# The tail of a cross-attention and mixture-of-experts kernel: four additions made into steps of their own, and the routing of two token groups moved up

## What is computed

```python
x = x + xattn(ctx, layernorm(x))          # 16 heads of 64, 1101 keys for each of 2 sequences of 1024
h = layernorm(x)                          # 2048 tokens of 256
shared = silu(h @ sg) * (h @ su) @ sd     # hidden width 512
# routing: l2-normed h against 8 group and 32 expert centroids
_, top_group_idx = top_k(group_scores, 4)
top_scores, top_idx = top_k(masked, 4)
gates = softmax(top_scores)
pos = cumsum(onehot, axis=0)[..., flat_e] - 1     # place of a token in its expert's list, capacity 320
buf[e, pos] = h[tok]
out_e = (silu(buf @ wg) * (buf @ wu)) @ wd        # 32 experts
routed[tok] += out_e * gate
out = x + shared + routed
```

## Time and profile before

| what | value |
|---|---|
| median of 3 runs | 1611.84 us (1609.86 to 1613.97) |
| the profiled execution | 1614.24 us, span 1612.5 us |
| mean granted TensorE clock | 0.984 |
| TensorE busy (matmuls) | 1503.6 us, 93% |
| VectorE busy | 1043.6 us, 65% |
| ScalarE busy | 796.2 us, 49% |
| POOL busy | 940.4 us, 58% |

### The profile page before, as it was taken

How to read it: one execution, slowest core, us unless ns; L and a number is a source line. 1 busy time by engine, 2 the same in 40 slices (tenths; PEclk the granted TensorE clock), 3 DMA queues, 4 the chain that set the end, 5 groups by cost and what they waited for, 6 DMA issues and landing times.

```text
span 1612.5 us, 23811 instructions
## 1 busy us (share of the span) xinstructions
PE 1503.6 (93%) x8086; PEld 1059.1 (66%) x8086; DVE 1043.6 (65%) x1574; ACT 796.2 (49%) x1501; POOL 940.4 (58%) x751
## 2 busy tenths in 40 slices
PE   4799999999999999999999999988989999999995
PEld 4465665555655665566555565546889999999995
DVE  6557556676676665767767776556756666666662
ACT  3455445444554455444554445433436666666663
POOL 4567756666677676765768768882534333343333
PEclk9999999999999999999999999998999999999998
DMA  3034430000000000000001011002256666666664
GB/s 107 11 81 96 101 81 15 10 15 10 25 15 10 15 11 24 15 11 15 24 18 32 24 41 33 31 31 69 87 172 189 178 168 176 182 189 180 168 177 90
DMA packets 99282, 117.93 MB, mean 73 GB/s; under 512 B 10595, under 2 KB 78181, under 8 KB 99173
## 3 DMA queue, kind: packets, MB, share of 16 engines
q1 hardware_dynamic: 82149, 96.97, 20.6%
q0 software_dynamic: 17056, 19.97, 6.3%
HBM read 74.93 MB, written 35.06 MB: 68 GB/s over the span
## 4 chain that ended last, share of the span: by engine, by line
PE 75%; DVE 16%; POOL 3%; ACT 3%; issue 2%; DMA 1%; SPq 0%; DVEq 0%; POOLq 0%; ACTq 0%
PE ps_o L965 14%; PE ps_t L822 9%; PE ps_m L822 8%; PE ps_m L927 8%; PE ps_st L822 7%; DVE arena_r L1325 7%; PE ps_st L950 6%; PE ps_st L954 6%; PE ps_m L859 3%; PE ps_o L859 3%; PE ps_t L985 2%; PE ps_t L1032 2%; PE ps_t L972 2%; DVE arena L1336 2%; POOL arena L762 2%
## 5 line engine op out<-in xcount | busy, mean ns | idle before, releaser
L762 POOL TENSOR_TENSOR arena<-arena 128x512 f32<-128x512 f32 (+1 forms) x512 | 660.8, 1292 | 321.7 <-ACT arena L1608 284.0
L1608 ACT ACTIVATE arena<-ps_st 128x512 f32<-128x512 f32 (+1 forms) x576 | 330.0, 597 | 457.5 <-PE ps_st L954 444.8
L1325 DVE TENSOR_REDUCE arena_r<-ps_m 128x1 fp32r<-128x1107 f32 x256 | 334.1, 1305 | 189.2 <-PE ps_m L927 187.0
L797 POOL DMA_INDIRECT acc_rows<-arena,ids x96 | 150.8, 1570 | 268.2 <-ACT arena L1671 240.5
L965 PE MATMUL ps_o<-arena 128*64 128x512 f32 (+1 forms) x1152 | 275.2, 603 | 0.0
L950 PE MATMUL ps_st<-arena_r 128*128 128x512 f32 (+1 forms) x576 | 246.3, 428 | 2.7 <-ACT arena L1608 2.6
L954 PE MATMUL ps_st<-arena_r 68*128 68x512 f32 (+2 forms) x576 | 230.8, 401 | 3.2 <-DVE arena_r L1332 2.1
L927 PE MATMUL ps_m<-arena_r 128*128 128x370 f32 x768 | 190.7, 357 | 36.4 <-DVE arena_r L1325 32.6
L927 PEld LDWEIGHTS ps_m<-arena_r 128*128 128x128 f32 x768 | 131.0, 191 | 102.2 <-DVE arena_r L1325 84.0
L950 PEld LDWEIGHTS ps_st<-arena_r 128*128 128x128 f32 (+1 forms) x576 | 106.6, 185 | 102.3 <-ACT arena L1608 68.2
L822 PE MATMUL ps_m<-arena_r 128*128 128x320 f32 (+1 forms) x864 | 165.2, 327 | 2.1 <-DVE arena_r L1415 1.2
(11 more groups left out here) (212 smaller groups left out, 1860.1 us busy)
## 6 DMA issues: line engine op xcount, KB each, us to landing
arena<-in_L_ffn_wg_dram SPq DMA_DIRECT2D x32, 512.0 KB, 4.6
arena<-in_L_ffn_wu_dram SPq DMA_DIRECT2D x32, 512.0 KB, 6.0
arena<-in_L_ffn_wd_dram SPq DMA_DIRECT2D x32, 512.0 KB, 3.9
x_slots<-route SPq DMA_DIRECT2D x5, 2176.0 KB, 12.9
arena<-x_slots SPq DMA_DIRECT2D x32, 272.0 KB, 2.7
arena_r<-arena_r SPq DMA_DIRECT2D x30, 275.2 KB, 3.6
arena<-in_L_xattn_Wkv_dram SPq DMA_DIRECT2D x32, 128.0 KB, 2.4
arena<-x_slots SPq DMA_DIRECT2D x32, 68.0 KB, 2.4
```

Of the source, the lines that this page charges most:

```text
L762: pool.tensor_tensor(total, probsT[0:rows, h, 0, :] if kt == 1 else total, probsT[0:rows, h, kt, :], ALU.add).then_inc(added, 1)
L797: pool.indirect_dma_start(out=dst[:, :], in_=y_sb[par][:, c, 0:w], in_offset=None, compute_op=ALU.add, out_offset=bass.IndirectOffsetOnAxi ...
L1325: dve.tensor_reduce(neg[h][:, c:c + 1], ps_m[:, :, 0:PIECE_W], AX.XY, ALU.max, negate=True)\
L1608: act.activation(probsT[0:rows, h, kt, :], ps_st[0:rows, n % 2, :], ACT.Exp).then_inc(exp_done, 1)
```

## The change

The four additions of a chunk become events `acc c,i` of their own, placed by hand in the list. For group 2, everything from `top` to `places_b` moves up; the norm of group 3 and its transposes move ahead of chunk 0's `down`; the additions of chunk 0 stand between routing steps of group 2; `pos` of group 2 now comes ahead of `score` of group 3. For group 3, `gexp`, `hot_*`, `pos`, `gates`, `places_*` and the scatters move ahead of chunk 1's `down`. No instruction is added or taken away. The code, with the long lists cut to two lines:

```diff
+    def sums(c):
+        return [("acc", c, i) for i in range(4)] + [("accout", c)]
+
-    def last(c):
+    def last(c, between=[]):
         return [("high", c, HIDS - 1), ("lowh", c, HIDS - 1)] + \
                ([("up", c + 1, 0), ("silu", c + 1, 0), ("hid", c + 1, 0)] if c < NCHUNKS - 1 else []) + \
-               [("down", c), ("accout", c)]
+               between + [("down", c)] + sums(c)
...
+             ("pos", 2), ("low", 3, 0), ("low", 3, 1), ("silu", 1, 0), ("acc", 0, 0), ("acc", 0, 1), ("gates", 2),
+             ("acc", 0, 2), ("places_a", 2), ("acc", 0, 3), ("accout", 0), ("places_b", 2), ("norm_c", 3),
...
+    tail += last(1, [("pos", 3), ("gates", 3), ("places_a", 3), ("places_b", 3)] + scats[3]) + hidden(2, 1)
...
-                if kind == "down":
-                    for i in range(4):
-                        jn = JOB["y", a, i]
-                        job_filled(dve, jn)
-                        t = a * GT + i
-                        dve.tensor_tensor(x_sb[:, t, :], bank_of(jn)[:, 0:D], x_sb[:, t, :], ALU.add)\
-                           .then_inc(free_of(jn), 1)
+                if kind == "acc":
+                    jn = JOB["y", a, ev[2]]
+                    job_filled(dve, jn)
+                    t = a * GT + ev[2]
+                    dve.tensor_tensor(x_sb[:, t, :], bank_of(jn)[:, 0:D], x_sb[:, t, :], ALU.add)\
+                       .then_inc(free_of(jn), 1)
```

More of the change, by code:

```diff
@@ L260, in whole_plan @@
                  ("hid", 0, 1), ("up", 0, 2), ("score", 2)] + outs
[L261 to L272, removed]
+    tail += [("silu", 0, 2), ("high", 0, 0), ("lowh", 0, 0), ("scored", 2), ("top", 2), ("hid", 0, 2), ("ws", 2), ("wl", 2),
+             ("stat_a", 3), ("stat_b", 3), ("up", 0, 3), ("root", 3), ("high", 0, 1), ("lowh", 0, 1),
+             ("mask_a", 2), ("mask_b", 2), ("silu", 0, 3), ("high", 0, 2), ("lowh", 0, 2), ("hid", 0, 3),
+             ("best_a", 2), ("best_b", 2), ("high", 0, 3), ("lowh", 0, 3), ("hot_a", 2), ("hot_b", 2), ("hot_c", 2),
+             ("gexp", 2), ("norm_a", 3), ("norm_b", 3), ("up", 1, 0), ("turned", 3, 0), ("turned", 3, 1), ("down", 0),
+             ("pos", 2), ("low", 3, 0), ("low", 3, 1), ("silu", 1, 0), ("acc", 0, 0), ("acc", 0, 1), ("gates", 2),
+             ("acc", 0, 2), ("places_a", 2), ("acc", 0, 3), ("accout", 0), ("places_b", 2), ("norm_c", 3),
+             ("hid", 1, 0), ("up", 1, 1)] + scats[2]
@@ new lines, in whole_plan @@
+    tail += [("silu", 1, 1), ("high", 1, 0), ("hid", 1, 1), ("lowh", 1, 0), ("score", 3), ("up", 1, 2), ("scored", 3),
+             ("top", 3), ("silu", 1, 2), ("high", 1, 1), ("hid", 1, 2), ("lowh", 1, 1), ("mask_a", 3), ("mask_b", 3),
+             ("up", 1, 3), ("best_a", 3), ("best_b", 3), ("silu", 1, 3), ("high", 1, 2), ("hid", 1, 3), ("lowh", 1, 2),
+             ("gexp", 3), ("hot_a", 3), ("hot_b", 3), ("hot_c", 3)]
+    tail += last(1, [("pos", 3), ("gates", 3), ("places_a", 3), ("places_b", 3)] + scats[3]) + hidden(2, 1)
```

## The result

| kernel | median | runs |
|---|---|---|
| before | 1613.24 us (1609.86 to 1614.14) | 8 |
| changed | 1618.25 us (1615.47 to 1621.28) | 8 |

The ratio is 1.0031, with a 95% interval from 1.0021 to 1.0040: the change makes the kernel 5.0 us slower, where 1612.6 us, in the range 1607.5 to 1617.5, had been forecast. The profiled execution took 1619.15 us, span 1617.4, at a mean clock of 0.982.

A forecast was written before the change was run, and what follows sets the result against it. Rows and TensorE's queue were taken to meet at the tail-to-loop seam, rows 1.96 us late. `erow` +3.4, clock -0.4 and -2.2 gave +0.8 us on 1611.84: 1612.6 us, range 1607.5 to 1617.5.

The forecast's parts named there:

- the bound of the seam: Between tail and expert loop: rows come 1.96 us after TensorE's chunk 3, so earlier scatters win only that plus clock effects.
- Up to the transposes of group 3: Tail, before `turned 3`: TensorE idles 9.9 us, to 1121.8, waiting for VectorE's `norm_b 3`, with 1.1 for a POOL hold-up.
- `turned 3`, `down 0`, `pos 2`: Tail, after the 9.9 us gap: clock at 0.50 for 5.5 us (bounds 4.0 and 7.3), work done at 1131.9.
- T: Time at which TensorE ends `pos 2`, behind `turned 3` and `down 0`: forecast as 1131.9.
- From there to `down 1`, and `pos 3`: Tail: TensorE waits 4.3 us ahead of `pos 3`, lower clock 5.5 us, `up 2,1` at 1158.5, 6.3 us later.
- To the seam: From `up 2,1` to the expert loop: TensorE's chunk 3 ends at 1191.6, rows already there at 1185.3.
- The seam: Tail to expert loop: `erow` 3.4 us later, full clock saving 0.4 and 2.2, in all +0.8 us.
- the clock at 1.00 in the first expert: Named sign at the loop's start: no wait for rows at `erow`, and the granted clock at 1.00.
- The base: Whole kernel: the +0.8 us was put on the median 1611.84, giving 1612.6 us.
- The faster one: Tail: rows were the bound, TensorE not held up, `up 2,1` by 1152.23; 1606.3 us, or 1609.3 within bounds; chance 0.14.
- the slower rival: VectorE at `top 2`: CAST held up to 2.4 us by POOL, clock low 7.3 us; 1616.4 to 1617.7; chance 0.14.
- the clock should be full: At `erow`: with no gap ahead, 0.4 us less there, and 4.5 us at half clock become 2.25.

The follow-up runs named there:

- Experiment 1: Changed kernel, with SP issuing the second expert's gate and up weights right behind the first expert's: 1613.72 us, ratio 1.0005 to the kernel before.
- experiment 2: Kernel before, with the second expert's gate and up weights issued early, right behind the first expert's: 1612.98 us, ratio 0.9994.
- experiment 4: Changed kernel, with 36 matmuls that nothing reads added in TensorE's gap ahead of `turned 3`: 1615.8 us, ratio 1.0013 to the kernel before.
- experiment 5: Changed kernel, with `down 0` ahead of `turned 3`, chunk 0's additions between group 2's `hot` steps and group 3's norm behind them: 1610.63 us, ratio 0.9989.

## Why the prediction was wrong

*What bounds the kernel, and the bound of the seam.* Right: two chains meet there, TensorE's and that of the rows. What it left out is a third that meets them a few microseconds later, the weights of the second expert. They belong to the loop, "whose work the change leaves alone"; but SP issues them behind chunk 3's last addition, so the tail sets when they start.

*Up to the transposes of group 3.* Right: 9.64 us against 9.9, with `hid 0,3` at 1113.03 (1113.5) and a hold-up of the CAST by POOL (1.07 us for an instruction that takes 0.17 at 1118.68 of the kernel before, so 0.9; 1.1 was taken).

*`turned 3`, `down 0`, `pos 2`.* Right: the lower clock lasts 5.9 us (mean 0.55 over 6.56, worked out as above) against 5.5, and `up 1,1` starts at 1131.06 where T was 1131.9. Some 0.4 of the difference is that this execution entered the tail earlier (group 2's second four transposes at 1097.53 against 1097.90).

*From there to `down 1`, and `pos 3`.* Right: 4.17 against 4.3, the clock low for 5.7 us against 5.5, `up 2,1` at 1157.60 against 1158.5.

*To the seam.* Right: chunk 3's last matmuls end at 1190.4 against 1191.6, and the rows don't hold `erow` up. Some 0.4 of the 1.2 is again the earlier entry. The rows were earlier than said, since the scatters took 1.29 us each rather than 1.43. (The working speaks of 32 steps of 1.43; its 1179.4 is 31, which is the right count for 32 scatters.)

***The seam.* This is the step that failed.** It counted +3.4 for the later `erow`, -0.4 and -2.2 for the clock that stays up once the wait for rows is gone, +0.8 in all. The first two came about as +2.05 and -0.22 (1190.27 and 1.32 us against 1188.22 and 1.54), and the loop's first batch did run at clock 1.00; but of the signs that were named, "the clock at 1.00 in the first expert" held only to about 1202. But the -2.2 took for granted that TensorE, faster now, would find everything there. The first expert became not 2.2 us shorter but 3.25 longer, because the half clock and the wait for rows had been the cover for the weights' landing. Without that cover the load is 2.41 us late for ScalarE and TensorE stands 2.11 us; then, in the profiled execution, the clock falls, 3.3 us more. Experiment 1 shows it: with that load moved and nothing else, 1613.72 against 1613.76 for the kernel before. The prediction asked what comes late next only of the rows, not of what SP issues behind them. It could have been read ahead from the profile of before: issue at 1187.76, use at 1194.93, of which some 2 us of the wait for rows and 2.2 of half clock were to be taken away, while SP's issue moves later with chunk 3.

*The base.* The sum was put on 1611.84, the median of 3 runs; over 8 runs it is 1613.24. Of the 5.65 us between 1612.6 and 1618.25, 1.4 is this. The other 4.2 is the failed step, 5.45 in the profiles (+3.25 in place of -2.2), less the 1.2 by which the first two terms came out lower than counted.

*The rivals.* The faster one did not come about: TensorE was held up, and reached `up 2,1` at 1157.60 and not by 1152.23. The time of the slower rival is near the measured one, but not its mechanism: the CAST of `top 2` was not held up. The rule of the Trainium skill (SBUF — State Buffer, Who interferes with whom) that spoke for it agrees with the trace in two other places: the CAST of 1.07 us and the step of 1.40 us in `mask 2`, each beside a POOL instruction of about 1.27. At `top 2` VectorE came first, at 1107.20 against 1107.40; that this decided it is read off the two start times, and no run moved them.

*What stays open.* Whether the clock falls behind the wait for the weights is not the same in all profiles (below), so the 3.3 us is that of one execution, and that the wait made the clock fall is not shown; the removal of wait and clock together is worth 4.5 us by the medians. The profile of before is one execution too: in that of experiment 2, whose tail has the same order, it is 88.54 us from group 2's second half of transposes to `erow` (1100.30 to 1188.84) against 90.32 (1097.90 to 1188.22), so a shift read against one profile is good to about 2 us.

## What to carry to other kernels

When a wait goes away, ask of every queue that ran on during it what it got done meanwhile, and compare for each load the time from issue to use with its time to land: here 7.2 us became 3.4, against 5.80. A load that waits in an in-order queue behind a result is a prefetch (it lands before it is needed) only as long as something else is late. And an order that is good for one chain (places and scatters early) is paid for where another engine must wait for it: with the routing of group 2 moved up, but each of the two long matmul blocks left ahead of the step that TensorE would wait for, the kernel gained 6.6 us where the whole change lost 5.0.

## What the runs showed of the hardware

A wait of about 2 us at the same place had two prices. In the changed kernel TensorE idled 2.11 us and the granted clock was at 0.50 from about 1202 on (mean 0.59 over the next 8.08 us); in experiment 4 it idled 2.00 us, and the clock stayed at 1.00, as this window of it shows:

```profile
1199.27:1206.60 7.33, 7.12 (x59) 6.26 (x59) 5.87 (x14) 4.10 (x10) 0.00 (x0) 1.00 0.41 132
```

The first expert took 17.91 us in the one and 14.90 (1191.70 to 1206.60) in the other; why the clock fell in one alone is open. Shorter waits show the same. In the kernel before, the clock was at 0.50 from 1117.00 on and the 24 matmuls of `down 0` behind a wait of 2.12 us took 4.94; in experiment 2, with the same order there, they ran at clock 1.00:

```profile
1122.10 3.07 PE L861 MATMUL ps_t<-arena_r 128*128 128x256 f32 x24 [2.33 <-DVE x_sb L1437]
```

And in experiment 5, where TensorE came to the first expert without a wait for rows and with none longer than 1.24 us, the clock fell to 0.50 by 1188; in experiment 1 it stayed at 1.00 behind the same 1.24. So "the clock should be full" with no gap ahead of `erow` is a chance and not a certainty.

Matmuls whose result nothing reads, set into an idle gap of 9.64 us, kept the clock at 1.00 behind it and were worth some 2.5 us.
